# Cross-attention and feed-forward: the q pair directly behind the k tile on TensorE, and both LayerNorm biases made by GpSimd beside rstd

## What is computed

```
for x, ctx of each of the 16 blocks:
    xh = layernorm(x)                                   # over 1024 columns
    q  = softmax over each head's 64 channels of (Wq @ xh) * 64**-0.5
    k  = softmax over the 1024 positions of (Wk @ ctx)  # 8 heads of 64 channels
    v  = Wv @ ctx
    context = k @ v.T per head;  o = Wo @ (context.T @ q) + bo
    x1 = x + o / ||o|| * g * sqrt(128)
    h  = layernorm(x1)
    query = h @ Wq2.T;  scores -> the 8 best of 256 slots -> softmax -> values
    gate  = sigmoid(w * clip(uncertainty(h)) + b)       # Wu1, gelu, Wu2, variance
    out   = x1 + h + gate * (values @ Wvd.T @ Wvu.T)
```

## Time and profile before

| | |
|---|---|
| median of 3 runs | 654.61 us (654.23 to 655.77) |
| the profiled execution | 655.03 us, of which the recorded span is 653.2 us |
| busy in the span | TensorE 621.8 us (95%), VectorE 578.9 (89%), ScalarE 419.2 (64%), GpSimd 374.8 (57%) |
| chain that ended last | TensorE 43%, VectorE 29%, issue 20%, ScalarE 3%, GpSimd 2%, DMA 2% |
| granted TensorE clock | 0.992 of 2.4 GHz over the span |

### The profile page before, as it was taken

How to read it: one execution, slowest core, us unless ns; L and a number is a source line. 1 busy time by engine, 2 the same in 40 slices (tenths; PEclk the granted TensorE clock), 3 DMA queues, 4 the chain that set the end, 5 groups by cost and what they waited for, 6 DMA issues and landing times.

```text
span 653.2 us, 11771 instructions
## 1 busy us (share of the span) xinstructions
PE 621.8 (95%) x3974; PEld 544.4 (83%) x3974; DVE 578.9 (89%) x788; ACT 419.2 (64%) x844; POOL 374.8 (57%) x291
## 2 busy tenths in 40 slices
PE   4899999999999999999999999999999799999896
PEld 3778888888888888888888888888889799998574
DVE  5999899999999999999999999999996746866896
ACT  5575666676676666767666666666664766583783
POOL 3945464747464646565656565564555667652394
PEclk9999999999999999999999999999999899999898
DMA  8833434343434343434344343433234100000056
GB/s 297 234 97 112 138 101 131 103 133 102 134 101 133 105 133 101 135 97 134 102 138 136 113 126 103 129 101 98 73 101 138 41 1 2 1 1 1 33 219 265
DMA packets 52011, 72.57 MB, mean 111 GB/s; under 512 B 10112, under 2 KB 42400, under 8 KB 51696
## 3 DMA queue, kind: packets, MB, share of 16 engines
q1 hardware_dynamic: 51056, 69.38, 35.5%
q0 software_dynamic: 896, 2.45, 1.2%
HBM read 29.85 MB, written 8.39 MB: 59 GB/s over the span
## 4 chain that ended last, share of the span: by engine, by line
PE 43%; DVE 29%; issue 20%; ACT 3%; DMA 2%; SPq 2%; POOL 2%; DVEq 0%; ACTq 0%; POOLq 0%
PE gm L476 8%; DVE qsum L1109 7%; DVE qm L1099 7%; PE ob L499 7%; PE gm L551 4%; PE turn L551 4%; DVE nkm L1078 3%; DVE st L1064 3%; DVE qs_sb L1102 3%; DVE st L1124 3%; PE turn L507 2%; PE q_slot L434 2%; PE k_slot L434 2%; PE k_slot L436 2%; DVE kt L1085 2%
## 5 line engine op out<-in xcount | busy, mean ns | idle before, releaser
L954 POOL TENSOR_TENSOR qs_sb<-qs_sb,qrec 128x1024 f32<-128x1024 f32 x64 | 122.0, 1907 | 206.6 <-DVE qrec L1113 206.6
L731 ACT ACTIVATE ek<-k_slot,nkm 128x1024 f32<-128x1024 f32 x62 | 69.0, 1114 | 101.1 <-DVE nkm L1078 101.0
L499 PE MATMUL ob<-mt_sb,q_hd 128*128 128x128 f32 x1024 | 127.3, 278 | 3.7 <-POOL mt_sb L960 3.1
L499 PEld LDWEIGHTS ob<-mt_sb,q_hd 128*128 128x128 f32 x1024 | 122.6, 193 | 8.3 <-ACT q_hd L746 3.5
L476 PE MATMUL gm<-ekT,ctxT 128*128 128x256 f32 x512 | 118.2, 379 | 0.0
L476 PEld LDWEIGHTS gm<-ekT,ctxT 128*128 128x128 f32 x512 | 96.9, 189 | 14.9 <-DMA ekT<-kt 0.3
L741 ACT ACTIVATE qs_sb<-qs_sb 128x1024 f32<-128x1024 f32 x64 | 68.4, 1069 | 41.4 <-DVE qs_sb L1102 41.4
L1078 DVE TENSOR_REDUCE nkm<-k_slot 128x1 f32<-128x1024 f32 x62 | 74.2, 1197 | 14.0 <-PE k_slot L436 14.0
L1109 DVE TENSOR_REDUCE qsum<-qs_sb 128x16 f32<-128x1024 f32 x64 | 77.0, 1202 | 5.2 <-ACT qs_sb L741 5.2
L1102 DVE TENSOR_TENSOR qs_sb<-q_slot,qm 128x1024 f32<-128x1024 f32 x64 | 78.4, 1225 | 2.2
L1085 DVE STREAM_TRANSPOSE kt<-ek 128x1024 f32<-128x1024 f32 x64 | 78.6, 1227 | 0.2 <-ACT ek L731 0.2
(11 more groups left out here) (196 smaller groups left out, 1276.1 us busy)
## 6 DMA issues: line engine op xcount, KB each, us to landing
ekT<-kt SPq DMA_DIRECT2D x496, 64.0 KB, 2.0
ctx_in<-ctx_rows SPq DMA_DIRECT2D x16, 512.0 KB, 4.6
x_all<-x SPq DMA_DIRECT2D x16, 512.0 KB, 3.6
ctxT<-ctx_cols SPq DMA_DIRECT2D x16, 512.0 KB, 4.1
out<-q_hd SPq DMA_DIRECT2D x15, 512.0 KB, 2.6
Wuq_in<-Wuq_cols SPq DMA_DIRECT2D x1, 1280.0 KB, 5.4
x_all<-values_cols POOLq DMA_DIRECT2D x1, 1024.0 KB, 7.2
ekT<-kt POOLq DMA_DIRECT2D x16, 64.0 KB, 3.8
```

The lines of the kernel that those rows point to most:

```text
L499: last = nc.tensor.matmul(ob[:, (j % 4) * C:(j % 4 + 1) * C], q_hd[:, t, j * P:(j + 1) * P], mt_sb[:, b % 2, t, :], start=(t == 0), stop=( ...
L954: nc.gpsimd.tensor_tensor(e, e, qrec[:, i % 2, :].unsqueeze(2).broadcast_to([P, PAIR, DH]), ALU.mult).then_inc(q_mul, 1)
```

## The change

Two things are done. TensorE's step is now `k_tile`, `q_pair`, `q_turn`, then the rest as before: the pair moves ahead of the turn, in all rounds. And the two biases leave VectorE: GpSimd makes each of them right behind the rstd it belongs to, as two instructions (mean times rstd into mr, then times -1 into nb) in place of one. Only the bias of block 0 stays on VectorE. VectorE gets one wait for the last rstd2 where `scale_bias(B - 1)` stood.

```
@@ TensorE
                     if b == 1 and i == 1:
                         value_products(1)
                         router_product()
+                    if has(p):
+                        if p == 0 and i == 0:
+                            pe.wait_ge(q_weights, 2)
+                            pe.wait_ge(k_exp, 4)
+                        q_pair(p, i)
+                        if p == 0 and i == 0:
+                            value_products(0)
                     qb, qi = (p, i - 2) if i >= 2 else (o, i + 2)
                     if has(qb):
...
                         q_turn(qb, qi)
                     if has(p):
-                        if p == 0 and i == 0:
-                            pe.wait_ge(q_weights, 2)
-                            pe.wait_ge(k_exp, 4)
-                        q_pair(p, i)
-                        if p == 0 and i == 0:
-                            value_products(0)
                         if p > 0 and i == 0:
                             g_part(p, 0, range(0, 4))
@@ GpSimd, rstd_pow(b)
-                wait(pool, x_nb, b)
                 nc.gpsimd.tensor_scalar(ve[:, :], mv1[:, 1:2], LN_EPS, None, ALU.add).then_inc(x_ve, 1)
                 pool.wait_ge(x_ve, b + 1)
                 nc.gpsimd.tensor_tensor(rstd[:, :], ve[:, :], half_neg[:, 0:1], ALU.pow).then_inc(x_rstd, 1)
+                if b > 0:
+                    pool.wait_ge(x_rstd, b + 1)
+                    nc.gpsimd.tensor_tensor(mr[:, :], mv1[:, 0:1], rstd[:, :], ALU.mult).then_inc(x_mr, 1)
+                    pool.wait_ge(x_mr, b)
+                    nc.gpsimd.tensor_scalar(nb[:, :], mr[:, :], -1.0, None, ALU.mult).then_inc(x_nb, 1)
@@ GpSimd, rstd2_pow(b)
+                pool.wait_ge(rstd2_done, b + 1)
+                nc.gpsimd.tensor_tensor(mr2[:, :], mv2[:, b, 0:1], rstd2[:, b, :], ALU.mult).then_inc(mr2_done, 1)
+                pool.wait_ge(mr2_done, b + 1)
+                nc.gpsimd.tensor_scalar(nb2[:, b, :], mr2[:, :], -1.0, None, ALU.mult).then_inc(nb2_done, 1)
@@ VectorE
-            x_bias(0)
+            x_bias()
...
                         if has(p):
                             k_scale(p)
-                        if 0 < b < B:
-                            x_bias(b)
-                        if has(e - 1):
-                            scale_bias(e - 1)
...
-            scale_bias(B - 1)
...
+            dve.wait_ge(rstd2_done, B)
             V.tensor_tensor(varh[:, :], mv2[:, :, 1], rstd2[:, :, 0], ALU.mult).then_inc(varh_step, 1)
```

More of the change, by code:

```diff
@@ L95, in attention_ffn_kernel @@
         nb = sb("nb", [P, 1])
+        mr = sb("mr", [P, 1])
+        mr2 = sb("mr2", [P, 1])
         att = ExitStack()
@@ L249, in attention_ffn_kernel @@
         x_rstd = sem("x_rstd")
+        x_mr = sem("x_mr")
         x_nb = sem("x_nb")
@@ L293, in attention_ffn_kernel @@
         rstd2_done = sem("rstd2_done")
+        mr2_done = sem("mr2_done")
         nb2_done = sem("nb2_done")
@@ L1068, in x_statistics, with x_bias @@
                 V.bn_aggr(mv1[:, :], st1[:, :]).then_inc(x_mv, 1)
-            def x_bias(b):
-                dve.wait_ge(x_rstd, b + 1)
-                wait(dve, x_norm, b)
+            def x_bias():
+                dve.wait_ge(x_rstd, 1)
                 V.scalar_tensor_tensor(nb[:, :], mv1[:, 0:1], -1.0, rstd[:, :], ALU.mult,
@@ L1126, in statistics @@
                 V.bn_aggr(mv2[:, b, :], st2[:, :]).then_inc(mv2_done, 1)
[L1128 to L1132, removed]
             def hT_low(b, k):
```

## The result

The changed kernel takes **658.63 us** (median of 6 runs, 658.4 to 660.77). The kernel before took 654.25 us in the same comparison (6 runs, 653.39 to 655.77). The ratio is 1.0074, with a 95% interval from 1.0058 to 1.009: slower by 0.7%, forecast 0.5%. The profiled execution took 658.43 us, with a span of 656.6 us (653.2 before). In the busy table VectorE fell from 578.9 to 549.6 us and GpSimd rose from 374.8 to 387.8.

What follows compares the result with a forecast made beforehand. VectorE was taken to pace the 31.24 us rounds by 0.54 us. Twelve rounds at +0.16 (+1.9), round 3 +0.70 and round 2 +0.87 gave +3.5 on 654.61: 658.1 us, 0.5% slower, range 654.0 to 660.5.

Steps and rivals of the forecast that it cites:

- The second loop: From step 3's k tile (T) through nkm, qsum, qrec, q_scale, x_low to step 0's pair: T + 8.69, a 0.57 us wait.
- The new round: Steady round after the change: 8.69 + 20.97 + 0.87 (turn) + 0.87 (o_turn) = 31.40 us, against 31.24 before.
- the rival of a free weight load: Group behind the turn, steps 0 to 2, pays nothing for its load: -3.5 us, 654.6, no difference; chance 0.14.
- Part 1, cost 0: Moving nb and nb2 from VectorE to GpSimd costs 0 and takes 1.87 + 0.15 us per round off VectorE.
- The rival of kscale: In step 1, nb's stall passes to VectorE's kscale: +6.5 us, 664.5; chance 0.05.
- the first loop: T, VectorE's work through steps 3, 0 and 1, step 2's pair, next T; paced rounds by 0.54 us, would stop binding.
- 0.38 to spare: Step 1's pair: VectorE's subtraction of step 0 is ready at 336.31, TensorE there at 336.69, so no wait.
- my first rival: TensorE sets the pace, x_low doesn't bind: rounds of 30.70 plus a few hundredths, 648.6 to 649 us; chance 0.08.
- The end, taken as 0: Behind T of round 15, the later turn and the feed-forward stage were each forecast to add 0 us.
- my two bounds: Most the end could add: 0.9 us for the turn behind the pair, 0.7 for GpSimd's queue.
- up to +0.7: Feed-forward stage: TensorE's second wait for ScalarE grows by up to 0.7 us, as GpSimd's queue gets two instructions more.
- two bounds of opposite sign: Feed-forward stage: up to -0.8 us without nb2 on VectorE, up to +0.7 from GpSimd's queue; taken as 0.

Runs made afterwards that it cites:

- The first experiment: Both biases made by GpSimd, TensorE's order left as before (turn, then pair), against the kernel before: 648.14 us, ratio 0.9892.
- the fastest version: Changed kernel with x_low ahead of q_scale in step 3 and VectorE's block statistics behind q_shift in step 0: 646.78 us, 646.45 when run again.

## Why the prediction was right

**The second loop and its bare length: right.** x_low at T + 8.69 was forecast and is there. So is the wait, though the rows print 0.44 where 0.57 were lost: the modelled end of the last k product hides part of it, as it did with the 0.29 in the earlier trace rows.

**The new round: right, 31.40 forecast, 31.37 measured.** The terms hold one by one: round 2 from T to T 30.52 (29.66 + 0.87 = 30.53), round 3 31.40, a turn with g_part behind it 0.87 (333.46 - 332.59). This also settles the rival of a free weight load, which needed 0.79. The sentence that the prediction quoted for it, from the section on the array's architecture of "TensorE: Matmul & The Clock Gate" in the Trainium skill, says that the queue can pull weight loads ahead. Behind these short transposes the trace shows little of it: the load for g_part begins at 333.36, 0.10 us ahead of its product, where loads behind a 512-column product begin 0.23 ahead.

**Part 1, cost 0: right for the rounds.** The first experiment has the four instructions on GpSimd and a round of 30.74, against TensorE's 30.70. The rival of kscale fell: it took 0.17 us in every one of the 16 rounds.

**The check on the first loop: right, and it held more than I saw.** "0.38 to spare" in step 1 is 0.37 in the trace. But the sentence rested on the wait of 0.57 in the step before. I used it as a check that passes and didn't ask what happens without that wait: it is a third loop of 31.1 us, nearly as long as the second. It changed nothing in the forecast. It is why my first rival was wrongly priced: had x_low come in time, the round would have been 31.1 and not 30.70 plus a few hundredths, and the time 651.5 (measured with x_low first), not 649.

**The end, taken as 0: wrong by 1.09 us.** It falls inside my two bounds (0.9 for the turn, 0.7 for GpSimd's queue), but my reason for 0 fails. The turn's 0.86 was mostly absorbed, as argued, in ScalarE's wait for Wuq (0.65 us in place of the 1.08 of the earlier trace rows); 0.33 are left at the last q_scale of GpSimd, counted from T of round 15. Then its two added instructions for nb2 put the sums of x and h back by another 0.57. The rows of before and of after (T at 476.92 and 479.23):

```profile
519.69 2.39 POOL L980 TENSOR_TENSOR x_all<-x_all,hbuf 128x1024 f32<-128x1024 f32 x1
...
526.11 4.76 POOL L980 TENSOR_TENSOR x_all<-x_all,hbuf 128x1024 f32<-128x1024 f32 x2
```

```profile
522.43 0.19 POOL L987 TENSOR_TENSOR mr<-mv,rstd 128x1 f32<-128x1 f32 x1
522.71 0.23 POOL L989 TENSOR_SCALAR nb<-mr 128x1 f32<-128x1 f32 x1
522.90 2.42 POOL L993 TENSOR_TENSOR x_all<-x_all,hbuf 128x1024 f32<-128x1024 f32 x1
...
529.35 7.23 POOL L993 TENSOR_TENSOR x_all<-x_all,hbuf 128x1024 f32<-128x1024 f32 x3
```

In both kernels VectorE's product with Wu2 runs into the second sum of the last row and is done just behind its end, at T + 54.23 before and at T + 55.14 now. ScalarE waits for it ahead of its copy, and TensorE for the copy. First before, then after, the product and TensorE's wait:

```profile
530.18 0.97 DVE L1154 TENSOR_TENSOR units<-units,Wu 128x256 f32<-128x256 f32 x1 [0.51 <-ACT units L788]
...
532.31 2.02 PE L499 MATMUL ob<-mt_sb,q_hd 128*128 128x128 f32 x16 [0.55 <-ACT o_sb L753]
```

```profile
531.86 2.51 DVE L1161 TENSOR_TENSOR units<-units,Wu 128x256 f32<-128x256 f32 x1 [0.51 <-ACT units L793]
...
535.53 2.02 PE L503 MATMUL ob<-mt_sb,q_hd 128*128 128x128 f32 x16 [2.10 <-ACT o_sb L758]
```

So the pair behind the wait begins at T + 56.30 in place of T + 55.39, 0.91 later, which is the 0.33 and the 0.57. The remaining 0.18 of the 1.09 come later, and their cause is open. The wait itself grew by more, from 0.55 to 2.10, because TensorE came to it 0.64 earlier (the turn ahead of it is at T + 53.17 in place of T + 53.81, after an output pair of 2.02 us in place of 2.92). That gains nothing, as the sum decides. It also means that the length of this wait isn't a price: the kernel with nb2 alone on VectorE, which has neither the order nor the two instructions for nb2, waits 2.0 us there and still begins its pair at T + 55.54.

That the 0.57 belongs to the two instructions shows in all the kernels: from the last q_scale to the row of sums it is 9.26 to 9.29 us in the five where VectorE makes nb2, and 9.83 to 9.87 in the eight where GpSimd makes it ahead of the first sum.

The prediction had named this queue ("up to +0.7") and then taken the middle of two bounds of opposite sign. The failed step is the claim that nb2's absence from VectorE gives back what GpSimd's two instructions take. VectorE was not late there: nb2's 1.82 us fell into time in which it then waited for ScalarE.

**The total: nearer than its parts.** Between the two profiles it is 3.4 us, forecast 3.5. But the rounds gave 3.1 of it (0.86 + 0.70 + 1.56), the end added 1.09, and 0.81 went off at the start, where x happened to arrive earlier. That these make 3.4 is luck; the medians differ by 4.4.

**A term that was missing: the clock in round 2.** The wait there became 2.15 us and TensorE's clock sometimes falls behind it (below). In the profile of the comparison it did not.

## What to carry to other kernels

The price of moving a piece of work is the waits that it covered where it stood, so list every loop that passes through that engine and how far each is from binding; a check that passes "with 0.4 to spare" because of a wait just before it is a loop of its own. When a small instruction is slow, look at what runs beside it before moving it to another engine: here moving it ahead of two other instructions on its own engine gained as much, and added nothing to GpSimd's queue at the end. Two changes that meet in one pipeline need to be timed apart: one of these was worth -6.4 us, the other +10.8 on top of it, and together they looked like a small loss. And a wait that gets shorter proves nothing by itself: look at whether what stands behind it starts earlier.

## What the runs showed of the hardware

**Some VectorE instructions wait out a whole GpSimd instruction, however small they are.** nb, one number per partition, took 1.87 us beginning 0.07 us after a q_scale of 1.92 us, and 0.14 us with GpSimd idle; nb2 in the same place took 1.70 on average. The product with Wu2, 128 x 256, took 0.42 us where GpSimd was idle, 0.97 where it met the last 0.69 us of a sum, and 2.51 where it began 0.10 us into one. All of these read two tiles of SBUF. Others are not held: the aggregate of the statistics (128 x 2, one tile read) began at 302.37, inside the q_scale of 301.27 to 303.17, and took 0.21 as elsewhere, and the subtraction, whose first input lies in PSUM, took 1.23 at 326.14 inside the q_scale of the earlier trace rows. kscale, which started at 308.67, one hundredth of a microsecond ahead of the q_scale, took 0.17 in all kernels; whether its start or its single input spares it, no run here separates. A start just ahead does seem to be enough: nb2 in the earlier trace rows, which reads two tiles, began 0.02 us ahead of GpSimd's next instruction (310.56) and took 0.15. Here "GPSIMD Engine Reference" of the Trainium skill, section 1 (Specifications), says that GpSimd shares the SBUF interface with VectorE, with contention for VectorE instructions with two SBUF inputs or in a two-port mode. The traces agree, and show its size here: not a slowdown by a share, but the rest of GpSimd's instruction.

**A wait of 2.15 us can cost more than itself.** In round 2 the changed kernel's pair of step 0 waits 2.15 us (1.17 before), since the turn no longer stands ahead of it. In the profile of the comparison the granted clock stayed at 1.00 behind it. In the second profile of the same kernel, and in that of the order alone, it fell to the lower of the two levels, 1.2 GHz, for part of the next stretch. The stretch from 51 to 54 us, first of the changed kernel, then of its second profile (busy us of PE, PEld, DVE, ACT, POOL, clock, DMA):

```profile
51.00:54.00 3.00, 3.00 (x21) 2.75 (x20) 2.93 (x6) 1.02 (x2) 2.57 (x3) 1.00 0.38 93
```

```profile
51.00:54.00 3.00, 3.00 (x13) 2.67 (x12) 2.93 (x6) 0.94 (x3) 2.12 (x3) 0.56 0.39 92
```

TensorE is busy throughout in both, but got through 21 matmuls in the one and 13 in the other; the turn took 1.91 us in place of 1.04:

```profile
51.57 1.91 PE L464 MATMUL turn<-ident,qs_sb 128*128 128x128 f32 x8
53.27 2.63 PE L480 MATMUL gm<-ekT,ctxT 128*128 128x256 f32 x8
```

From the pair to the next k tile are 7.46 us (49.98 to 57.44) in place of 5.83. So a wait of 2.15 to 2.18 us there was followed by the lower clock in three of the four profiles that had it (the third is that of nb2 behind the sum), at 1.5 to 1.6 us each; the kernels with a wait of 1.2 us or none there kept 1.00 in this stretch in their profiles. The wait's length alone doesn't decide: behind the wait for mt_bias at the end of attention the output pair took 2.02 us after a wait of 3.12 in one kernel (nb2 alone on VectorE) and 3.48 after the same 3.12 in another (nb2 back ahead of qsum), at a granted clock of 1.00 and of 0.50 in its first 2 us. The lower clock of round 2 may be why the changed kernel's runs lie in two groups, four from 658.40 to 658.63 and two at 660.69 and 660.77, but runs without a profile don't show it. "TensorE: Matmul & The Clock Gate" of the Trainium skill, part 1, says that the array's clock has two levels set by how busy the array has been, and that the moment of a change varies between runs; the rows agree with both.

**The order of the change is a few hundredths cheaper where nothing waits.** From a k tile to g_part the fastest version takes 3.69 us in step 1 (113.78 to 117.47), the kernel with the turn ahead in that step 3.73 (114.71 to 118.44): a pair directly behind its k tile took 1.36, below the 1.39 that I had from the earlier trace rows. Over the four steps that goes toward its round of 30.62, under the 30.70 that I had taken as TensorE's floor, and may be part of why the changed kernel's is 31.37 and not 31.40.
